# The carry chain of a blocked cumulative sum placed earlier, and its cumsum tiles spread over three PSUM banks

## What is computed

```python
xn = layernorm(x)
keys   = quaternions(xn @ Wk.T + bk); keys = keys / norm(keys)
values = quaternions(xn @ Wv.T + bv)
bound  = quat_mul(values, keys)
memory = cumsum(bound, axis=sequence)          # 4096 positions
retrieved = quat_mul(memory, conj(keys)) / sqrt(position)
normed = layernorm(retrieved) * ln_g + ln_b
x = x + xn + (normed @ Wo.T + bo)
```

## Time and profile before

| | us |
|---|---|
| timed runs, median of 2 | 7372.3 (7367.33 to 7377.28) |
| the profiled execution | 7362.28 |
| its span on the slowest core (core 5) | 7360.7 |
| spans of the 8 cores | 7336.9 to 7360.7 |
| stage C's set-up, about 4324 to 4440 | 116 |
| stage C's blocks, about 4440 to 6046 | 1606 |

### The profile page before, as it was taken

How to read it: one execution, slowest core, us unless ns; L and a number is a source line. 1 busy time by engine, 2 the same in 40 slices (tenths; PEclk the granted TensorE clock), 3 DMA queues, 4 the chain that set the end, 5 groups by cost and what they waited for, 6 DMA issues and landing times.

```text
span 7360.7 us, 60776 instructions; the slowest of 8 cores (7336.9 to 7360.7 us)
## 1 busy us (share of the span) xinstructions
PE 4866.8 (66%) x21328; PEld 2056.2 (28%) x21328; DVE 1795.3 (24%) x2926; ACT 2085.6 (28%) x2542; POOL 328.8 (4%) x229
## 2 busy tenths in 40 slices
PE   2376868677686876398889923444444433888998
PEld 2222323222232322144344411111111111434443
DVE  3312121212212122411111124444444442111111
ACT  1143636345363534122122202121111111212221
POOL 0000000000000000000000001111111100000000
PEclk9998978889898888599999956666666666999999
DMA  3201010110101011400100050000000014010000
GB/s 77 53 1 32 1 32 1 32 32 1 32 1 32 1 32 40 116 23 26 43 24 24 26 168 0 23 23 23 9 20 20 20 58 171 26 44 24 23 26 32
DMA packets 84213, 256.12 MB, mean 35 GB/s; under 512 B 25797, under 2 KB 25797, under 8 KB 83146
## 3 DMA queue, kind: packets, MB, share of 16 engines
q1 hardware_dynamic: 51562, 222.34, 8.4%
q0 software_dynamic: 32352, 29.89, 3.0%
HBM read 196.10 MB, written 85.98 MB: 38 GB/s over the span
## 4 chain that ended last, share of the span: by engine, by line
PE 65%; DVE 16%; ACT 6%; issue 5%; DMA 4%; another core or an unknown queue 3%; DVEq 0%; POOL 0%; ACTq 0%; SPq 0%; POOLq 0%
PE psC L530 8%; PE psD L536 7%; PE psA L656 5%; PE psA L662 5%; PE psA L682 5%; PE psB L682 5%; PE psB L662 5%; PE psB L656 5%; PE psA L508 3%; DVE m L866 3%; DVE bcst L542 3%; PE psB L508 3%; PE psA L924 2%; PE psT L300 2%
## 5 line engine op out<-in xcount | busy, mean ns | idle before, releaser
L530 PE MATMUL psC<-PTb,Vt 128*128 128x512 bf16 x2048 | 831.7, 406 | 276.4 <-DVE O_st L544 232.0
L536 PE MATMUL psD<-PTb,ones2d 128*128 128x512 bf16 x2048 | 829.4, 405 | 0.0
L525 ACT ACTIVATE PTb<-psA,negc 128x1024 bf16<-128x1024 f32 x512 | 571.5, 1116 | 470.7 <-PE psA L508 470.6
L525 ACT ACTIVATE PTb<-psB,negc 128x1024 bf16<-128x1024 f32 x512 | 571.5, 1116 | 221.0 <-PE psB L508 220.9
L542 DVE RECIPROCAL bcst<-psD 128x512 f32<-128x512 f32 x64 | 214.9, 3358 | 1605.1 <-PE psD L536 1579.4
L293 ACT ACTIVATE ln_tm<-xb,nmr_all,rstd_all 128x1024 bf16<-128x1024 f32 x128 | 159.0, 1242 | 1279.1 <-DMA xb<-x3s 396.0
L300 PE MATMUL psT<-ident,ln_tm 128*128 128x128 bf16 x1024 | 129.4, 306 | 549.1 <-ACT ln_tm L293 391.9
L530 PEld LDWEIGHTS psC<-PTb,Vt 128*128 128x128 bf16 x2048 | 208.4, 102 | 825.9 <-issue 723.2
L508 PE MATMUL psA<-Q_all,K_fm 128*128 128x512 bf16 x1024 | 334.7, 411 | 0.0
L1062 PE MATMUL psT<-ident,zb 128*128 128x128 bf16 x256 | 32.4, 306 | 446.2 <-ACT zb L1056 446.2
L508 PE MATMUL psB<-Q_all,K_fm 128*128 128x512 bf16 x1024 | 322.9, 399 | 0.0
(11 more groups left out here) (216 smaller groups left out, 6480.9 us busy)
## 6 DMA issues: line engine op xcount, KB each, us to landing
xb<-x SPq DMA_DIRECT2D x64, 512.0 KB, 5.7
xb<-x1s SPq DMA_DIRECT2D x64, 512.0 KB, 4.2
xb<-x3s SPq DMA_DIRECT2D x64, 512.0 KB, 5.7
x1s<-xb SPq DMA_DIRECT2D x32, 512.0 KB, 2.8
x2s<-xb SPq DMA_DIRECT2D x32, 512.0 KB, 2.7
y<-xb SPq DMA_DIRECT2D x32, 512.0 KB, 2.7
xb<-x2s SPq DMA_DIRECT2D x20, 512.0 KB, 4.5
x3s<-xb SPq DMA_DIRECT2D x20, 512.0 KB, 2.6
```

The costliest lines, as they stand in the source:

```text
L525: p.op("scalar", lambda E, pt=pt, ps=ps: E.activation(pt[:, :], ps[:, :], AF.Exp, bias=negc[:, :], scale=1.0), reads=[ps, negc], writes=[p ...
L530: p.op("tensor", lambda E, pt=pt, mt=mt, mp=mp, half=half: E.matmul(psC[:, 0:512], Vt[:, mt * 130:mt * 130 + 128], pt[:, half * 512:half * ...
L536: p.op("tensor", lambda E, pt=pt, mp=mp, half=half: E.matmul(psD[:, 0:512], ones2d[:, :], pt[:, half * 512:half * 512 + 512], start=(mp == ...
```

## The change

`front_carry(pb + 1)` moves from behind `back_out(pb)` to ahead of it, directly behind `front_main(pb + 1)`. In `back_cumsum` the 8 pairs of matmuls of a block no longer alternate between psC and psD, but go round psC, psD and psE; the evacuations follow the same rule. No instruction is added or removed.

```diff
@@ back_cumsum
                     for u in range(4):
                         cb_, cbo = cbrow(pb, u)
                         for ds in range(2):
-                            psM = psC if ds == 0 else psD
+                            psM = [psC, psD, psE][(2 * u + ds) % 3]
                             p.op("tensor", lambda E, psM=psM, u=u, ds=ds, bb16=bb16: E.matmul(
@@ the loop
                     back_retr(pb)
                     if pb + 1 < 8:
                         front_main(pb + 1)
+                        front_carry(pb + 1)
                     back_out(pb)
-                    if pb + 1 < 8:
-                        front_carry(pb + 1)
```

## The result

The changed kernel is 0.25% slower: its time is 1.0025 of the kernel before, with a 95% interval from 1.0014 to 1.0037. On 7370 us that is 18 us, between 10 and 27. The forecast was +18.2 us.

The account below looks back on a forecast made before the run. Stage C was taken as one chain hopping between engines, none busy half the time. 12.61 - 7.81 - 2.20 = +2.60 us a pass over 7 passes gave +18.2 us, on 7372.3 a forecast of 7390.5 us, range 7364 to 7426.

Parts of the forecast that it names:

- The cost of the move: On DVE between `front_main`'s last product and `back_out`'s first `bn_stats`: 13.22 us in place of 0.61, +12.61 us a pass.
- The time taken away on PE: Behind `back_out`'s last bias matmul: the first cumsum matmul follows at +0.31 us in place of +8.12, -7.81 us a pass.
- The cumsum at the high clock: From first cumsum matmul to retrieval product: at the high clock ACT sets the pace, 7.40 us against 9.60, -2.20 a pass.
- How long the high clock would last: In the cumsum behind the output matmuls: the clock stays high 4.0 us, the last two tiles arriving about when ACT wants them.
- The cold rival: In the cumsum: one-row matmuls lower the clock at once, the -2.20 is gone, +4.80 us a pass, 7405.9 us; chance 0.19.
- The bound: On the cumsum's gain: 0 to 2.20 us a pass, since ACT's eight evacuations are a floor.
- The third bank: psE in the cumsum: worth nothing at the low clock, at most 0.2 us a pass at the high, within the -2.20.
- The phase of the clock: Within each tile's matmuls the moment the clock rises may shift: up to 2.3 us a pass, some 16 us.
- The hidden chain: Rival: the twelve DVE instructions ahead of `back_out` cost nothing, -10.01 us a pass, -70.1 us, 7302.2 us; chance 0.07.

Follow-up runs that it names:

- the interleaved kernel: Against the kernel before: carry chain cut into four rounds, one in each tile of `back_out`; three banks, cumsum directly behind `back_out`. Measured 0.992 (0.9898 to 0.9943).
- psE first: Against the interleaved kernel: the cumsum's banks go in the order psE, psC, psD. The one comparable run took 7297.2 us.
- the move alone: Against the changed kernel: `front_carry` moved, but the cumsum keeps two banks, psC and psD. One comparable run of 7398.2 us, 1.0052 of the kernel before.

## Why the prediction was right

**The cost of the move** was taken from pass 0 of the old trace, which had the new order already: 13.22 us priced, 13.23 measured. Its two parts, the chain and the wait, were told apart by the kernel that puts the chain behind tile 0 (9.4 us and the rest). That the place is what costs, and not the work, is shown by the interleaved kernel.

**The time taken away on PE**: 7.81 priced, 7.91 measured. Two of the seven passes of before needed 0.35 us more than the pass that I read.

**The cumsum at the high clock**: -2.20 priced, -2.08 measured. How long the high clock would last was only partly right. In four of the seven passes it lasted the 4.0 us that the earlier trace rows gave, and the last bank's worth came up to 0.25 us late behind its fall, where I had it just in time. In the other three it lasted over 5 us of the cumsum, in two of them to its last pair of matmuls, as in the pass shown under the phase of the clock. The cold rival (0.19) is out: one-row matmuls didn't take the clock down sooner than the near idleness of the earlier trace rows did. The bound, no more than 2.20, was too tight: with psE first it was 2.46 (9.60 to 7.14), since the wait for psD's residual add was no floor. The Trainium skill's account of a clock that oscillates while PSUM banks are cycled (TensorE: Matmul & The Clock Gate, "A second HAM failure mode: psum-queue depth-cycling") is shown by no run here: with three banks in the old order the kernel kept its time, 1.0004.

**The third bank** is the step that was wrong. I priced it at 0.2 us at most at the high clock, and a move with two banks shows 1.02. The slip has two parts. I compared two steady rates, 0.80 and 0.78 us a tile, but two banks came back slower than that: in the move alone the evacuations stand 0.78, 0.90 and 0.86 us apart, also because the second matmul of a pair takes 0.39 us to its end and not the 0.32 to the next start. And I left out that each delay leaves more matmuls behind the fall of the clock. The total didn't suffer, since the three-bank case was worked out step by step. The Trainium skill's rule on rotating banks (Perfetto Trace Analysis, "Matmuls"), which I had set aside by the rows at the low clock, agrees with the trace at the high clock: 8.54 us with two banks, 7.52 with three.

**The phase of the clock** was left at 0 in the sum, with up to 2.3 us a pass as its bound: 0.84 was measured. It is nearly the whole difference between the 18.2 us of the forecast and the 24.3 us by which the loop on core 2 grew. PE's order of time in the last tile of one pass, 15.5 us long where before has 13.7, then the last matmul of the cumsum behind it:

```profile
5347.70 3.57 PE L1074 MATMUL psC<-WgoT,lfZ 128*128 128x512 bf16 x8 [1.37 <-ACT lfZ L1068]
5351.73 2.83 PE L1074 MATMUL psD<-WgoT,lfZ 128*128 128x512 bf16 x8
...
5360.22 0.39 PE L1007 MATMUL psD<-csnapBb,onesC 1*128 1x512 bf16 x1
```

The kernel before needs 3.2 us for the first group and 1.90 for the second in such a tile. Here the clock rises only late in the second (0.50 in 5351.70 to 5352.70, 1.00 from 5353.70 on); in return the cumsum, begun at 5354.81, is at the high clock to its last matmul. This is not chance: passes 2 to 7 took 202.4, 201.5, 202.9, 201.5, 199.9 and 201.3 us on all four cores that can be compared, to within 0.1, and those of the kernel before agree to within 0.2 on seven of its eight cores. The phase repeats with the order of the instructions, and no row of before gave the new order's. The time's own interval holds both 18.2 and 24.3, so that it came out at the forecast's 18 is partly luck.

**The hidden chain** (0.07) didn't happen with this edit, since nothing stood in front of `bn_stats`; made true by the interleaving, it gave 59 us instead of 70, and the slow tiles of five passes, on average 1.66 us a pass, are 11.6 of the difference.

**Small slips.** PE's share in the earlier trace rows is 0.42, not 0.43. The 156.5 us of the earlier trace rows are of all 32 evacuations from psC, and not only of the first of each pass. And 18 us could be told from no change: the interval excludes 1.

## What to carry to other kernels

In a loop that is one chain over several engines, work moved off its end needs a gap in the queue that it is moved into: look for the engine's waits inside the neighbouring stage and cut the moved work to their size. Look in the trace for a place where the new order exists already, a first or last pass; its rows priced this cost to 0.01 us. And where the clock falls in the middle of a run of matmuls, as in the cumsum here, a delay of some tenths is paid again behind the fall, so a spare buffer that a comparison of rates calls idle can matter (here 1.02 us a pass).

## What was not expected of the hardware

Behind the output matmuls the granted clock stayed at 1.00 for some 4 us whether PE was nearly idle or issued 13 cumsum matmuls in that time; but in three of seven passes it stayed for over 5, those in which it had risen late. The pattern of slow and fast passes repeats from core to core and differs from kernel to kernel. Extra matmuls that nobody reads made a pass shorter, 181.2 us in place of 190.0, although PE had more to do in all.
